# Attention masks and positions on TensorE: one wide product where there were several narrow ones

## What is computed

```python
pos = jnp.cumsum(jax.nn.sigmoid(y).transpose(0, 2, 1), axis=-1)
relpos = pos[..., :, None] - pos[..., None, :]
causal = jnp.triu(jnp.full((i, i), NEG_BIG, dtype=x.dtype), k=1)
mask = causal - relpos
scores = jnp.einsum('bhid,bhjd->bhij', q / s, k / s) / np.sqrt(D_HEAD) + mask
attn = jax.nn.softmax(scores, axis=-1)
o = jnp.einsum('bhij,bhjd->bhid', attn, v)
```

## Time and profile before

| | |
|---|---|
| median of 3 runs | 1642.04 us (1635.63, 1642.04, 1642.19) |
| profiled execution, its own time | 1640.95 us |
| its span in the trace | 1639.2 us |
| mean granted TensorE clock | 0.959 of 2.4 GHz |
| TensorE products busy | 1410.5 us, 86% |
| TensorE weight loads busy | 1044.4 us, 64% |
| VectorE busy | 1153.5 us, 70% |
| ScalarE busy | 712.7 us, 43% |
| GpSimd busy | 434.8 us, 27% |

### The profile page before, as it was taken

The page is one execution under the profiler, slowest core; times in us unless marked ns, Lnnn a source line. Parts: engine busy times, 40 slices in busy tenths (PEclk is TensorE's granted clock), DMA queues, the critical chain, the costliest instruction groups (busy, mean ns, idle before and its releaser), DMA issues. The chain is left out here.

```text
span 1639.2 us, 68165 instructions
## 1 busy us (share of the span) xinstructions
PE 1410.5 (86%) x28603; PEld 1044.4 (64%) x28618; DVE 1153.5 (70%) x5594; ACT 712.7 (43%) x2475; POOL 434.8 (27%) x819
## 2 busy tenths in 40 slices
PE   5788888888888888888888887479999999999886
PEld 4677777777777777777777776245555556555443
DVE  5577777777777777777777776566576776776485
ACT  3333333333333333323333332126777776777764
POOL 2001111111111111111111111454345535522354
PEclk7899999999999999999999998568999999999998
DMA  5200000000000000000000000077636734742001
GB/s 120 28 4 5 5 5 7 5 5 7 5 5 7 5 5 7 5 5 7 5 5 7 5 5 6 12 158 120 70 71 104 100 62 83 101 70 33 1 14 39
DMA packets 68951, 53.86 MB, mean 33 GB/s; under 512 B 12686, under 2 KB 68390, under 8 KB 68646
## 3 DMA queue, kind: packets, MB, share of 16 engines
q1 hardware_dynamic: 66470, 49.32, 18.5%
q10 hardware_dynamic: 2176, 0.20, 0.1%
HBM read 31.84 MB, written 15.47 MB: 29 GB/s over the span
## 5 line engine op out<-in xcount | busy, mean ns | idle before, releaser
L739 PEld LDWEIGHTS PS<-GB,W 128*128 128x128 f16 x18432 | 505.3, 96 | 267.2 <-DVE GB L1058 261.7
L739 PE MATMUL PS<-GB,W 128*128 128x32 f16 x18432 | 556.1, 177 | 133.7 <-DVE GB L1058 124.5
L951 ACT ACTIVATE tr<-PS 128x16 f32<-128x16 f32 x512 | 93.8, 183 | 507.8 <-PE PS L739 507.8
L2400 DVE TENSOR_REDUCE MX<-PS 128x1 f32<-128x512 f32 (+3 forms) x352 | 219.7, 635 | 118.2 <-PE PS L1859 115.3
L2138 ACT ACTIVATE PT<-PS 128x512 f32<-128x512 f32 (+1 forms) x352 | 193.3, 566 | 120.0 <-PE PS L1875 115.7
L806 PE MATMUL PS<-W 128*128 128x256 f16 x1248 | 221.3, 273 | 0.0
L1044 DVE SCALAR_TENSOR_TENSOR u_<-tr,PS 128x16 f32<-128x16 f32 x512 | 87.3, 171 | 122.6 <-PE PS L739 108.9
L953 ACT ACTIVATE tz<-PS 128x16 f32<-128x16 f32 x512 | 93.7, 183 | 175.4 <-PE PS L739 175.4
L692 POOL TENSOR_TENSOR rt<-mv,eps 128x1 f32<-128x1 f32 x96 | 18.2, 189 | 547.8 <-DVE mv L1069 547.8
L1856 PE MATMUL PS<-KS,QS 99*128 99x256 bf16 (+3 forms) x512 | 134.6, 315 | 11.1 <-DVE MX L2400 9.3
L1051 DVE SCALAR_TENSOR_TENSOR zg<-tz,HR 128x16 f32<-128x16 f32 x512 | 90.5, 177 | 71.0 <-ACT tz L953 1.3
(11 more groups left out here) (396 smaller groups left out, 2550.6 us busy)
## 6 DMA issues: line engine op xcount, KB each, us to landing
QS<-q_parts SPq DMA_DIRECT2D x90, 128.0 KB, 11.8
KS<-k_parts SPq DMA_DIRECT2D x90, 128.0 KB, 14.7
q_parts<-PQ SPq DMA_DIRECT2D x16, 384.0 KB, 10.5
k_parts<-PK SPq DMA_DIRECT2D x16, 384.0 KB, 3.3
X<-XM SPq DMA_DIRECT2D x32, 64.0 KB
out_dram<-X SPq DMA_DIRECT2D x8, 256.0 KB, 2.3
XM<-in_L_attn_x_dram SPq DMA_DIRECT2D x16, 80.0 KB
s_hh<-in_L_attn_w_hh_dram SPq DMA_DIRECT2D x1, 768.0 KB, 5.6
```

The source lines that it names most:

```text
L739: return pe.matmul(bank[:, p, end - wide:end], W[:, kc, w:w + P], GBF[:, state - wide:state], start=False, stop=True, skip_group_check=True)
L951: act.activation(as_states(tr), now(pR), ACT.Tanh, scale=gate_scale).then_inc(hn_tr.sem, 1)
L2400: dve.tensor_reduce(MX[:, g % 2, heads[0]:heads[-1] + 1, NT - 1 - it], p_x[:, k % 2, 0:len(heads) * w].rearrange("p (a w) -> p a w", w=w), ...
```

## The change

**Masks.** For an item with two or four heads, one product adds the mask for all heads: the constant tile is read once per head by a broadcast, and the output is the diagonal block of each head, 128 columns out of each w. Items of one head are as before. Items of two heads lose one product for each mask, items of four lose three: 5 a group in max_item and 5 in exp_item, so 10 x 32 groups = 320.

**Positions.** The loop runs over the distance k of the tiles in place of the tiles t: for k = 0 the triangle times all four tiles (64 columns), for k = 1, 2, 3 the square of ones times the first 4-k tiles (48, 32, 16 columns), added to the last 4-k tiles. Ten products become four, 20 records 8. In the loop k = 0 stands at item 12, k = 1, 2, 3 stand at item 13, and item 14 has none. For eight sequences that is 48 products less.

BY_REDUCE and BY_SELECT are empty, so their tests always take the way with the mask.

```diff
+        BY_REDUCE, BY_SELECT = (), ()
...
-                    for t in {12: (0, 1), 13: (2,), 14: (3,)}.get(i, ()):
-                        if t == 0:
+                    for k in {12: (0,), 13: (1, 2, 3)}.get(i, ()):
+                        if k == 0:
                             pe.wait_ge(qk.sem, qk.value(pe, b, 3))
                             pe.wait_ge(sg.sem, sg.value(pe, b))
                         p_p = p_b[:, 0:NT * HEADS].rearrange("p (t h) -> p t h", t=NT)
-                        for k in range(t + 1):
-                            last = pe.matmul(p_p[:, t, :], (tri if k == t else ones)[:, :], SG[:, k, :],
-                                             start=(k == 0), stop=(k == t))
-                        if t == NT - 1:
+                        last = pe.matmul(p_p[:, k:, :], (ones if k else tri)[:, :], SG[:, 0:NT - k, :],
+                                         start=(k == 0), stop=(k == NT - 1), skip_group_check=True)
+                        if k == NT - 1:
                             last.then_inc(pos_ps.sem, 1)
...
                     pe.wait_ge(sg.sem, sg.value(pe, b))
-                    for t in range(NT):
-                        for k in range(t + 1):
-                            last = pe.matmul(PS[:, 3, t * HEADS:(t + 1) * HEADS], (tri if k == t else ones)[:, :], SG[:, k, :],
-                                             start=(k == 0), stop=(k == t))
+                    for k in range(NT):
+                        last = pe.matmul(PS[:, 3, k * HEADS:NT * HEADS], (ones if k else tri)[:, :], SG[:, 0:NT - k, :],
+                                         start=(k == 0), stop=(k == NT - 1), skip_group_check=True)
                     last.then_inc(pos_ps.sem, 1)
...
-                    for a, i in enumerate(heads):
-                        last = pe.matmul(bank[:, (a + 1) * w - P:(a + 1) * w], identb[:, :], maskU[:, :],
+                    if it not in BY_REDUCE:
+                        diagonal = bank[:, 0:len(heads) * w].rearrange("p (a w) -> p a w", w=w)[:, :, w - P:]
+                        last = pe.matmul(diagonal, identb[:, :], maskU[:, :].unsqueeze(1).to_broadcast([P, len(heads), P]),
                                          start=False, stop=True, skip_group_check=True)
...
-                    for a, i in enumerate(heads):
-                        last = pe.matmul(bank[:, a * w:a * w + P], identb[:, :], maskL[:, :],
+                    if j not in BY_SELECT:
+                        diagonal = bank[:, 0:len(heads) * w].rearrange("p (a w) -> p a w", w=w)[:, :, 0:P]
+                        last = pe.matmul(diagonal, identb[:, :], maskL[:, :].unsqueeze(1).to_broadcast([P, len(heads), P]),
                                          start=False, stop=True, skip_group_check=True)
```

More of the change, by code:

```diff
@@ L1855, in max_item @@
                     for a, i in enumerate(heads):
-                        pe.matmul(bank[:, a * w:(a + 1) * w], QS[0:KM, p, 4 * g + i, q], KS[0:KM, p, 4 * g + i, 0:w],
-                                  start=(a == 0), stop=False, skip_group_check=True)
-                    for a, i in enumerate(heads):
-                        last = pe.matmul(bank[:, (a + 1) * w - P:(a + 1) * w], identb[:, :], maskU[:, :],
+                        last = pe.matmul(bank[:, a * w:(a + 1) * w], QS[0:KM, p, 4 * g + i, q], KS[0:KM, p, 4 * g + i, 0:w],
+                                         start=(a == 0), stop=(it in BY_REDUCE), skip_group_check=True)
+                    if it not in BY_REDUCE:
+                        diagonal = bank[:, 0:len(heads) * w].rearrange("p (a w) -> p a w", w=w)[:, :, w - P:]
+                        last = pe.matmul(diagonal, identb[:, :], maskU[:, :].unsqueeze(1).to_broadcast([P, len(heads), P]),
                                          start=False, stop=True, skip_group_check=True)
@@ L1871, in exp_item @@
                     for a, i in enumerate(heads):
-                        pe.matmul(bank[:, a * w:(a + 1) * w], KS[0:KF, p, 4 * g + i, j * P:(j + 1) * P], QS[0:KF, p, 4 * g + i, j * P:S],
-                                  start=(a == 0), stop=False, skip_group_check=True)
-                    for a, i in enumerate(heads):
-                        last = pe.matmul(bank[:, a * w:a * w + P], identb[:, :], maskL[:, :],
+                        last = pe.matmul(bank[:, a * w:(a + 1) * w], KS[0:KF, p, 4 * g + i, j * P:(j + 1) * P], QS[0:KF, p, 4 * g + i, j * P:S],
+                                         start=(a == 0), stop=(j in BY_SELECT), skip_group_check=True)
+                    if j not in BY_SELECT:
+                        diagonal = bank[:, 0:len(heads) * w].rearrange("p (a w) -> p a w", w=w)[:, :, 0:P]
+                        last = pe.matmul(diagonal, identb[:, :], maskL[:, :].unsqueeze(1).to_broadcast([P, len(heads), P]),
                                          start=False, stop=True, skip_group_check=True)
```

## The result

| | before | after |
|---|---|---|
| median of 5 runs each, us | 1640.01 (1635.63 to 1642.19) | 1623.69 (1622.48 to 1627.88) |
| profiled execution, its own time | 1640.95 | 1622.48 |
| its span | 1639.2 | 1620.8 |
| mean granted clock | 0.959 | 0.969 |
| TensorE products, count | 28603 | 28187 |

The ratio is 0.9911, with an interval of 0.9888 to 0.9934: faster, and 1623.7 us lies just inside the range of 1623 to 1639. So the change is worth 0.6 to 0.9%. The profiled pair is 18.4 us apart, and the first thing to ask is how much of that is the change's.

What follows compares the result with a forecast made beforehand. The prediction took TensorE to bound the attention stage's middle; positions in the loop 3.9, masks 0.9, first two sequences 3.7 and clock 5.7 sum to 14.2 us off 1640.95, giving a median of 1628 us, range 1623 to 1639.

Steps and rivals of the forecast that it cites:

- What bounds the kernel: Middle of the attention stage: TensorE, busy 47.9 of 50 us, so work taken from it can shorten the stage.
- the walk: Items 12 to 15: ScalarE sets the pace, only item 14's last four positions products, 0.81 us, delay ready work.
- Positions in the loop: Six sequences: 1.26 us of TensorE's time saved in each, 0.65 carried on, 3.9 us in all (0 to 7.6).
- Masks: 32 groups: wide masks save 0.06 us a group, 1.9 us in all, half carried: 0.9 us (0 to 1.9).
- First two sequences: Positions of the first two sequences: 1.2 us saved in the first, 2.54 in the second, sum 3.7 (2.5 to 5.1).
- The clock: Loop: two clock falls behind narrow products and waits, 2.8 us each, would not come after the change: 5.7 us.
- The sum: Whole kernel: 14.2 us saved from the profiled 1640.95, median forecast 1628 us; chance of the forecast case 0.57.
- Not shortening: Rival, loop: VectorE and ScalarE pace the items, falls stay, only 3.7 us saved, 1638.3 us; chance 0.13.
- Falls as before: Rival, loop: both clock falls stay and the rest of the sum holds, 1633.5 us; chance 0.20.
- More falls: Rival, loop: a clock fall in all six sequences, four more costing 11.3 us, 1645 us; chance 0.05.
- Slow wide mask: Rival, masks: wide products stream at half rate, 27.5 us more, 1655 us; chance 0.05.
- Change doesn't do what it says: Rival, whole program: ruled out beforehand, as the order shows 368 products gone; given no chance.

Runs made afterwards that it cites:

- e7: The changed kernel with all four wide positions products moved to item 14; 1630.17 us, 0.9977 of before.
- e2: The kernel before with only the change's masks, positions still ten narrow products; 1636.67 us, 1.0019 of before.
- e1: The kernel before with only the change's positions, masks as before; 1626.87 us, 0.9969 of before.
- e0: The changed kernel again, unedited, with before beside it (the second measurement); 1626.24 against 1634.91 us, ratio 0.9943.
- e11: The changed kernel with VectorE's second multiply-add moved from item 14 to item 13; 1621.87 us, 0.9931 of before.
- e4: The kernel before with each narrow positions product in the loop issued twice; 1663.08 us, 1.0169 of before.
- e9: The changed kernel with all four wide positions products moved to item 16; 1628.68 us, 0.9966 of before.
- e12: The changed kernel with the second multiply-add at item 13 and all four positions products at item 16; 1627.29 us, 0.9958 of before.
- e10: The kernel before without any edit, a single execution for another profile; 1642.54 us.
- e5: The kernel before with its ten positions products in the loop made 64 columns wide, same places; 1631.92 us, 0.9988 of before.
- e8: The changed kernel with each mask of two or four heads added twice; 1651.10 us, 1.0102 of before.

## Why the prediction was right, and where not

**What bounds the kernel, and the walk** over items 12 to 14: right. e7 shows its core, that only the last 0.81 us are carried.

**Positions in the loop**, 0.65 of 1.26 us a sequence. The price of a record, 110 ns, measured 107 (0.64 / 6), and the eight take 0.28 + 0.64 = 0.92 us where 0.88 was written. The step that was off is the estimate that item 17 starts 0.6 to 0.7 us earlier: it is 0.80 or 0.21, by which of two operations that mostly start 0.04 us apart goes first. VectorE was named as late next, and rightly. The prediction took it that VectorE would get free of GpSimd's work by being earlier; it comes only as early as GpSimd, and then either can be held up. In after's four full periods the mean is 57.55 for 58.17, 0.62 with the masks, 0.49 without: 2.9 us over six sequences, where 3.9 was forecast. With 5 of 18 sequences at 0.80 and 13 at 0.21 it is 2.2.

**Masks**, 0.9: right in size, 0.13 us a sequence in the periods, but by luck. The 0.06 us a group came from differences of 0.01 us, and measured over the loop it is 0.018; the half that was taken to be lost isn't lost. Both steps were wrong and made up for each other. The Trainium skill (TensorE: Matmul & The Clock Gate, section "Back-to-back issue gap") puts 2.5 ns on a product beyond its columns; for 320 products that is an estimate of 0.8 us before any wait. The trace agrees roughly: 2 ns for one product less (115 and 113) and 5 ns for three (225 and 220), 0.6 us in all.

**First two sequences**, 3.7: measured 3.0. The second sequence's 2.54 measured 2.56. The step that failed is the first sequence's 1.2, of which 0.5 was found in this pair and nothing across the profiles (32.06 us with old positions in e2, 33.14 with new ones in e1): SyncE was taken to be done with its forerunner 24.8 us into the stage, as before. It was done at 25.5; six issues took 1.2 us more. That lengthening isn't bound to the change, as the same six take 3.53 us in e2. In e0, e1 and e11 one issue of q_parts<-PQ takes 1.68 to 1.91 us in place of 0.43, and L1563 stands 26.1 to 26.3 us into the stage. There the queue loses all that KAT gains. What lengthens its issues stays open.

**The clock**, 5.7: right for the pair of profiles, where two falls went and none came. It was wrong as a term of the median: falls come 0 to 3 times in an execution of before, at no fixed sequence, and the second measurement's clocks, 0.9669 and 0.9639, at 0.97 us for 0.001 make 2.9 us (with the GRU's gap in that line, so an upper guess for the loop). That narrow products bring falls is made likely by e4, in five of six sequences, but e4 has more of them and more time besides. The prediction's reason, that falls come out of the stretch thick with narrow products and waits, holds in its second half by e9 and e12, where the clock falls at items 12 to 14 without a product for positions. What the profiles bear out is the length: 6.8 us or more in all ten falls of before, e10 and e4 in the loop, 3.4 us in all seven of the kernels with wide products. Which of the waits and the narrow products starts a fall stays open. That the width of the columns matters rests on one profile and the spread of e5, with a ratio that takes in no effect. The Trainium skill's rule that falls follow from gaps in which TensorE idles (the same page, section "HAM oscillation — how this bites in real kernels") doesn't describe the falls of before and e4: TensorE is busy 4.00 of 4 us in the slices before and after the one in which e4's clock falls. The falls of e9 and e12 do come in or behind waits of 0.74 to 1.02 us. By that rule the prediction's rival kept both falls at 1633.5 us; the median of 1623.7 and the profile without a fall speak against it. The second measurement alone would not: its difference of 8.7 us is what this rival had, 8.5.

**The sum.** By the profiles: 3.0 ahead of the loop, 5.7 for falls, 2.8 in the loop and 1.3 behind it, 12.8 for the forecast's 14.2. The first measurement's medians are 16.3 apart, and the forecast of 1628.0 is 4.3 above 1623.7. That this comes from what the change didn't touch, the gap in the GRU and the falls of the executions that happened to be drawn, is likely but not shown, as one execution of each was profiled in that measurement. Beside e0 before stands at 1634.9, and the difference is 8.7. There 7.1 us (12.8 - 5.7, some tenths of it clock) and 2.9 of clock make 10.0, inside the ratio's interval (5.4 to 13.1 us). So both times lie inside the range, but of the 14.2 us forecast the second measurement finds some 9, and that the first finds 16 is in part the luck of which executions were drawn.

**Rivals.** Not shortening: out, by the periods. Falls as before: open in its cause, as said, but the long ones didn't come in three profiles. More falls: out, as three profiles of the changed kernel have none, none and two short ones in the loop. Slow wide mask: out, 0.11 and 0.22 us. Change doesn't do what it says: out, 416 records less in TensorE's count (320 + 96).

## What to carry to other kernels

Find the item where work stands in front of other work that is ready; only there is a product's time worth taking away, and an experiment that moves all of it to that one item (e7) prices it. When the last wait is on an engine that another can hold up, look at the order of their starts: 0.04 us decided here over 0.6 us a sequence, and moving one of them out of the way (e11) made it sure. A price that is the difference of two rows of one digit is better read over all the places where it occurs: 0.06 us a group was 0.018. And an edit that is worth a fall or two of the clock is measured by many executions and their clocks, never by one pair of profiles.

## What the runs showed of the hardware beyond what was expected

- An fp32 product with 16, 48 or 64 columns on 128 partitions takes the same time, 101 to 107 ns a record (e5 and after), two records each.
- The granted clock can fall in the middle of a stretch of narrow fp32 products (e4: four records in 0.44 us, then two in 0.43 and four in 0.85), with one wait of 0.38 us as TensorE's only idle time in the 8 us around it, and it does so in some executions and not in others. It can fall at the same items without such products, in a wait of 1.02 us (e9, e12).
- A VectorE multiply-add of 128x511 in fp32 and a GpSimd subtraction of 128x512 take turns: 0.75 and 1.16 us when undisturbed, and the one that comes second is lengthened to 1.74 or 1.72 us, though both are listed as running. At starts 0.03 to 0.04 us apart either can be the second (VectorE 13 times, GpSimd twice). The Trainium skill (GPSIMD Engine Reference, section "Specifications") has GpSimd share its way to SBUF with VectorE, with contention for VectorE instructions of two SBUF inputs. The trace agrees, as the multiply-add has two, and it adds the price: 0.99 us for VectorE and 0.56 for GpSimd, three quarters or more of the other's operation. GpSimd's cast beside the multiply-add gets longer too, 1.10 us for 0.61 (e11).
- SyncE's issue of DMAs isn't of fixed length: six issues of one kind took 2.77 to 4.21 us (e8 the most), one of another kind 0.43 to 1.91.
- All compute engines can stand still for 1 to 5 us behind a hole in the transfers of the queue "instruction": holes of 8.7 to 11.8 us in the six profiles with a gap, at most 7.0 in the eight without.
